# A dynamic-time-warp stage: distances by ScalarE's root and its remainder, rows moved by halves, and the next norm's statistics moved into it

## The reference

```python
def _pairwise_euclidean(a, b):
    aa = jnp.sum(a * a, axis=-1)[:, None]
    bb = jnp.sum(b * b, axis=-1)[None, :]
    ab = a @ b.T
    return jnp.sqrt(jnp.maximum(aa + bb - 2.0 * ab, 0.0))

# _dtw_cost: row i, column j
r = d_ij + jnp.minimum(jnp.minimum(up, left), diag)

# _align_one
expanded = jnp.zeros((T_large, d), dtype=small.dtype).at[j_idx].add(contrib)
```

## Time and profile before

| | |
|---|---|
| median of 3 runs | 1110.68 us (1107.84 to 1112.83) |
| the profiled execution's own time | 1109.92 us |
| its span | 1108.1 us |
| TensorE busy | 863.0 us, 78% |
| VectorE busy | 799.6 us, 72% |
| ScalarE busy | 571.4 us, 52% |
| GpSimd busy | 453.3 us, 41% |
| mean granted TensorE clock | 0.905 |

### The profile page before, as it was taken

One profiled execution on the slowest core, in us unless ns is written; L12 is line 12 of the kernel. 1 busy time (PEld: TensorE's weight loads), 2 busy tenths in 40 slices (PEclk: granted clock), 3 DMA queues, 4 the chain that ended last, 5 costly groups with the idle time before them and its releaser, 6 DMA issues. The chain is left out here.

```text
span 1108.1 us, 25980 instructions
## 1 busy us (share of the span) xinstructions
PE 863.0 (78%) x10175; PEld 617.1 (56%) x10175; DVE 799.6 (72%) x1846; ACT 571.4 (52%) x1299; POOL 453.3 (41%) x288
## 2 busy tenths in 40 slices
PE   4174399689648787179877989898898989868888
PEld 3052254678526566125555767676676767644457
DVE  4889786778764333868879678586958777788964
ACT  3062154467524333456766574647465574346774
POOL 4001130487326665558503363433335262608710
PEclk9687699899759999589989999899999999998989
DMA  5321000400241111200010000000000000000001
GB/s 150 98 62 77 0 1 1 158 2 2 68 161 44 43 44 42 73 1 1 2 49 1 26 2 25 2 25 3 25 4 25 15 13 3 3 1 2 1 2 38
DMA packets 27125, 35.92 MB, mean 32 GB/s; under 512 B 7835, under 2 KB 20444, under 8 KB 26238
## 3 DMA queue, kind: packets, MB, share of 16 engines
q1 hardware_dynamic: 21310, 27.84, 7.9%
q0 software_dynamic: 2496, 5.12, 1.7%
q10 hardware_dynamic: 3200, 1.31, 0.5%
HBM read 26.98 MB, written 7.27 MB: 31 GB/s over the span
## 5 line engine op out<-in xcount | busy, mean ns | idle before, releaser
L1787 PE MATMUL soft_expert_ps<-soft_W,soft_slots 128*32 128x128 f32 x4096 | 139.1, 279 | 14.8 <-issue 8.6
L2058 DVE TENSOR_TENSOR soft_outs<-soft_expert_ps,soft_bias 128x512 f32<-128x512 f32 x128 | 87.2, 687 | 77.2 <-PE soft_expert_ps L1787 77.1
L1787 PEld LDWEIGHTS soft_expert_ps<-soft_W,soft_slots 128*32 128x32 f32 x4096 | 107.2, 111 | 47.2 <-issue 43.3
L925 POOL TENSOR_TENSOR l_prob<-l_prob,l_inv 128x1024 f32<-128x1024 f32 x48 | 91.3, 1901 | 53.4 <-DVE l_inv L1069 53.0
L1879 ACT ACTIVATE soft_slots<-soft_slot_ps 128x512 f32<-128x512 f32 x128 | 69.3, 593 | 81.6 <-PE soft_slot_ps L1773 79.8
L1960 POOL TENSOR_TENSOR l_ring<-l_ring,soft_inv 128x1024 f32<-128x1024 f32 x15 | 39.0, 2629 | 109.4 <-DVE soft_inv L2051 57.7
L1054 DVE TENSOR_REDUCE l_under<-l_score 128x16 f32<-128x1024 f32 x48 | 58.4, 1217 | 32.3 <-PE l_score L1132 14.4
L952 PE MATMUL l_turned<-ident,l_prob 128*128 128x128 f32 x384 | 56.4, 293 | 20.7 <-POOL l_prob L925 20.6
L1736 PE MATMUL soft_slot_ps<-phi,xnT 128*128 128x256 f32 x256 | 66.0, 415 | 7.5 <-ACT soft_spread L1867 5.6
L1960 POOL TENSOR_TENSOR soft_spread<-soft_spread,soft_inv 128x1024 f32<-128x1024 f32 x16 | 41.3, 2610 | 74.0 <-DVE soft_inv L2051 74.0
L1801 PE MATMUL soft_mix_ps<-soft_outs,soft_combT 128*64 128x128 f32 x1024 | 70.0, 279 | 1.5 <-DVE soft_acc L2074 1.5
(11 more groups left out here) (429 smaller groups left out, 2198.2 us busy)
## 6 DMA issues: line engine op xcount, KB each, us to landing
moe_w<-in_moe_W SPq DMA_DIRECT2D x2, 2048.0 KB, 10.0
soft_W<-in_soft_W SPq DMA_DIRECT2D x16, 256.0 KB, 2.7
kept<-early SPq DMA_DIRECT2D x1, 2048.0 KB, 6.3
l_keys<-in_moe_b SPq DMA_DIRECT2D x1, 2048.0 KB, 8.5
l_asked<-kept SPq DMA_DIRECT2D x1, 2048.0 KB, 13.2
ctxT<-in_ctxT SPq DMA_DIRECT2D x1, 1024.0 KB, 5.3
moe_rows<-xn_tok SPq DMA_DIRECT2D x4, 256.0 KB, 3.7
expert_rings<-moe_back SPq DMA_DIRECT2D x4, 256.0 KB, 5.4
```

The source lines that it names most:

```text
L925: nc.gpsimd.tensor_tensor(prob[t % 4][:], prob[t % 4][:], inv[t % 2][:].unsqueeze(2).broadcast_to(S16), ALU.mult).then_inc(share_done, 1)
L1787: last = nc.tensor.matmul(expert_ps[c][32 * j:32 * j + 32, h, tt, :], slots[u % 3][:, h, tt, 128 * c + 32 * j:128 * c + 32 * j + 32], W[i ...
L2058: nc.vector.tensor_tensor(outs[u % 3][:, c].rearrange("p h t d -> p (h t) d"), expert_ps[c][:].rearrange("p h t d -> p (h t) d"), bias[i % ...
```

## The change

- The matmuls that open the banks take bf16 operands.
- ScalarE clamps the distances (relu with scale -2), takes the root and squares the root. VectorE no longer clamps or floors, and has no reciprocal: it gets the inverse of the root from its bits by an integer multiply-add and a refining step, and corrects the root by what its square leaves of the distance, all half by half.
- The minimum for the scan's reset is made ahead of the rows, into a tile of its own. The stop mask is written to `leave`.
- The path's mask is made in two halves of eight tiles, and TensorE waits for the half it needs. A group of four tiles is moved into one whole bank, with four banks for four groups, and added in one operation over 128 partitions.
- The statistics of the next norm are taken behind each group's addition, in `warp`. `bit_ffn` takes one root, one reciprocal and one shift for all 16 tiles.
- For the first four tiles of `bit_ffn`, VectorE instead of GpSimd takes the lift off.

```diff
+INVERSE = float(0x7EF311C3)
...
             for k in range(2):
+                own = slice(8 * k, 8 * k + 8)
+                act.wait_ge(dist_done, k + 1)
+                nc.scalar.activation(dist2[:, own, :], dist_ps[k][:], ACT.Relu, scale=-2.0).then_inc(dist2_done, 1)
                 act.wait_ge(dist2_done, k + 1)
-                nc.scalar.activation(root[:, 8 * k:8 * k + 8, :], dist2[:, 8 * k:8 * k + 8, :], ACT.Sqrt).then_inc(root_done, 1)
+                nc.scalar.activation(root[:, own, :], dist2[:, own, :], ACT.Sqrt).then_inc(root_done, 1)
+                act.wait_ge(root_done, k + 1)
+                nc.scalar.activation(square[:, own, :], root[:, own, :], ACT.Square).then_inc(square_done, 1)
...
-                    nc.tensor.matmul(dist_ps[k][S * h:S * h + S], core.zero[:].broadcast_to([128, S]), ctxT[:, 0:512],
-                                     start=True, stop=False)
+                    nc.tensor.matmul(dist_ps[k][S * h:S * h + S], core.zero[:].bitcast(BF16)[:, 0:1].broadcast_to([128, S]),
+                                     core.ident16[:].unsqueeze(1).broadcast_to([128, 4, 128]), start=True, stop=False)
...
-            pe.wait_ge(path_done, 1)
             for g in range(G):
+                pe.wait_ge(path_done, g // 2 + 1)
                 for k in range(4):
                     t = 4 * g + k
-                    if k == 0 and g >= 2:
-                        pe.wait_ge(added, 2 * g - 2)
                     for h in range(2):
                         half = slice(S * h, S * h + S)
-                        last = nc.tensor.matmul(moved[2 * (g % 2) + h][half, k, :], path[half, t, :], core.ctx_tok[half, t, :],
+                        last = nc.tensor.matmul(moved[g][half, k, :], path[half, t, :], core.ctx_tok[half, t, :],
                                                 start=True, stop=True)
...
+                s, a, q, r, c = (tile[:, own, :] for tile in (root, dist2, square, inv, cost))
                 dve.wait_ge(root_done, k + 1)
-                nc.vector.tensor_scalar_max(inv[:, half, :], root[:, half, :], 1e-30).then_inc(floor_done, 1)
-                dve.wait_ge(floor_done, k + 1)
-                nc.vector.reciprocal(cost[:, half, :], inv[:, half, :]).then_inc(inv_done, 1)
-                dve.wait_ge(inv_done, k + 1)
-                nc.vector.tensor_tensor(inv[:, half, :], dist2[:, half, :], cost[:, half, :], ALU.mult).then_inc(ratio_done, 1)
-                dve.wait_ge(ratio_done, k + 1)
-                nc.vector.tensor_tensor(cost[:, half, :], inv[:, half, :], root[:, half, :], ALU.add).then_inc(cost_done, 1)
+                nc.vector.tensor_scalar(bits(r), bits(s), -1.0, INVERSE, ALU.mult, ALU.add).then_inc(cost_step, 1)
+                dve.wait_ge(cost_step, n + 1)
+                nc.vector.tensor_tensor(c, s, r, ALU.mult).then_inc(cost_step, 1)
+                dve.wait_ge(square_done, k + 1)
+                nc.vector.tensor_tensor(q, q, a, ALU.subtract).then_inc(cost_step, 1)
+                dve.wait_ge(cost_step, n + 2)
+                nc.vector.scalar_tensor_tensor(r, c, 2.0, r, ALU.subtract, ALU.mult).then_inc(cost_step, 1)
+                dve.wait_ge(cost_step, n + 4)
+                nc.vector.tensor_tensor(c, q, r, ALU.mult).then_inc(cost_step, 1)
+                n += 5
+                dve.wait_ge(cost_step, n)
+                nc.vector.scalar_tensor_tensor(c, s, 2.0, c, ALU.mult, ALU.add).then_inc(cost_done, 1)
...
+            dve.wait_ge(dist_done, 2)
+            columns = core.columns[:].unsqueeze(1).broadcast_to([128, R, S])
+            nc.vector.tensor_scalar_min(cut, columns, 1.0).then_inc(first_cut, 1)
...
-            nc.vector.tensor_scalar_min(stops[:], columns, 1.0).then_inc(first_cut, 1)
...
+            for k in range(2):
+                own = slice(8 * k, 8 * k + 8)
+                columns = core.columns[:].unsqueeze(1).broadcast_to([128, 8, S])
+                nc.vector.tensor_tensor(within[:, own, :], columns, exits_ps[:, 1, own].unsqueeze(2).broadcast_to([128, 8, S]),
+                                        ALU.is_le).then_inc(within_done, 1)
+                nc.vector.tensor_tensor(path[:, own, :], columns, exits_ps[:, 0, own].unsqueeze(2).broadcast_to([128, 8, S]),
+                                        ALU.is_ge).then_inc(within_done, 1)
+                dve.wait_ge(within_done, 2 * k + 2)
+                nc.vector.tensor_tensor(path[:, own, :], path[:, own, :], within[:, own, :], ALU.mult).then_inc(path_done, 1)
             for g in range(G):
                 dve.wait_ge(moved_done, g + 1)
-                for h in range(2):
-                    half = slice(S * h, S * h + S)
-                    xs = core.x[half, 4 * g:4 * g + 4, :]
-                    nc.vector.tensor_tensor(xs, moved[2 * (g % 2) + h][half], xs, ALU.add).then_inc(added, 1)
+                xs = core.x[:, 4 * g:4 * g + 4, :]
+                nc.vector.tensor_tensor(xs, moved[g][:], xs, ALU.add).then_inc(added, 1)
+                dve.wait_ge(added, g + 1)
+                for t in range(4 * g, 4 * g + 4):
+                    last = nc.vector.bn_stats(stats[:, t, :], core.x[:, t, :])
+                last.then_inc(measured, 1)
+                dve.wait_ge(measured, g + 1)
+                for t in range(4 * g, 4 * g + 4):
+                    nc.vector.bn_aggr(core.bit_meanvar[:, t, :], stats[:, t, :])
...
-            for t in range(T):
+            for t in range(4, T):
                 pool.wait_ge(in_lifted, 5 * (t // 4) + t % 4 + 2)
...
-            deviate(0)
-            deviate(1)
+            nc.scalar.activation(std[:], meanvar[:, :, 1], ACT.Sqrt, bias=core.eps[:, 0:1]).then_inc(std_done, 1)
             normalise(0)
-            deviate(2)
-            deviate(3)
...
+            def settle(t):
+                dve.wait_ge(in_lifted, t + 2)
+                nc.vector.tensor_scalar(xs[:, t, :], lifted[:, t, :], ROUND, in_scale[:, t:t + 1], ALU.subtract, ALU.mult).then_inc(xs_done, 1)
...
-            statistics(0)
-            statistics(1)
+            dve.wait_ge(std_done, 1)
+            nc.vector.reciprocal(rstd[:], std[:]).then_inc(rstd_done, 1)
+            dve.wait_ge(rstd_done, 1)
+            nc.vector.scalar_tensor_tensor(shift[:], meanvar[:, :, 0], -1.0, rstd[:], ALU.mult, ALU.mult).then_inc(shift_done, 1)
             normalise(0)
             quantise(0)
-            statistics(2)
-            statistics(3)
+            for t in range(4):
+                settle(t)
             normalise(1)
             quantise(1)
```

54 lines of the change are left out of this document (15 added, 39 removed).

## The result

The changed kernel takes 1101.92 us (median of five runs, 1100.16 to 1104.62), beside 1110.2 us (1107.84 to 1112.83) for the kernel before: a ratio of 0.9927, 95% interval 0.9907 to 0.9947. The forecast was 1102.8 us. The profiled execution took 1100.28 us with a span of 1098.5 us, 9.6 us less than before; TensorE's mean granted clock was 0.913 beside 0.905.

A forecast was written before the change was run, and what follows sets the result against it. VectorE's chain was taken to bound most of 19 to 142 us, TensorE the `bit_ffn` loop after. Costs 4.05 + cut 0.7 − tail 0.2 + head 3.4 = 7.95 us off 1109.92; as a median 1102.8 us, range 1098.0 to 1107.0.

The forecast's parts named there:

- The bound: From 19 to 142 us one engine at a time, mostly VectorE, carries the chain; its shift carries to the end.
- Zeroing: Opening matmuls in bf16: half the passes go, worth 0.4 us before the first half of distances, 0.4 before the second.
- Relu, root, square: Distances on ScalarE: each operation takes 0.60 us, and the first root is there at 26.2 us.
- that rival: At the Relu: table loads of 1.28 us, two per half; gain 2.8, time 1104.0; chance 0.13 with fully serial collision.
- The costs: VectorE's cost stage: 3.75 us per half, ending at 35.85 with the collision; worth 4.05 us.
- The collision: VectorE's cost operations meet GpSimd's bias splits from 26.2 us on; 2.1 us lost.
- The rival without a collision: Cost stage: VectorE gets in first and GpSimd waits; 2.1 us more gain, 1100.7 us; chance 0.17.
- The bounds: Cost stage: the meeting with GpSimd loses between 0 and 2.8 us (all serial).
- The cut: The scan's minimum goes from behind the rows to under the wait for `mine` ahead of them; gain 0.7 us.
- The tail: From E, the interval masks' start, to the last aggregation: four groups end at E + 11.9; costs 0.2 us.
- The head: Start of `bit_ffn`: TensorE begins 4.8 us after the start instead of 8.2; gain 3.4 us.
- the third rival: Start of `bit_ffn`: TensorE's low clock gives back 1.7 to 3.4 us of the head; 1104.5 to 1106.2; chance 0.15.

The follow-up runs named there:

- e7_delay: Changed kernel with two more idle VectorE reciprocals (3.35 us each) ahead of the last cost operation; 1091.82 us, ratio 0.9968.
- e6_again: Repeat: changed kernel with GpSimd's memset behind its bias splits and statistics of groups 2 and 3 in `bit_ffn`; 1095.94 us, ratio 0.9867.
- e2_no_collision: Changed kernel with GpSimd's big memset moved behind its bias splits; 1099.69 us, ratio 0.9917.
- e3_stats_back: Changed kernel with all statistics of the next norm back in `bit_ffn`, in groups of four; 1102.55 us, ratio 0.9933.
- e4_split_statistics: Changed kernel with only groups 0 and 1 measured in `warp`, groups 2 and 3 in `bit_ffn`; 1099.37 us, ratio 0.9894.

## Why the prediction was right, point by point

- *The bound.* VectorE's chain to E and the head behind it set the time, and the shift passes on: e7_delay showed it with 6.5 us for 6.39. The loop of `bit_ffn` ran at its clock of 1.00 and passed the shift on.
- *Zeroing.* Expected 0.4 ahead of the first half and 0.4 more before the second. The second is 0.64; the first is 0.49 in one pair of executions, within a spread of 2.5 us, so it isn't shown. That most of it would be eaten by the collision wasn't in the sum. The first Relu at 24.93 (24.8) fits, by some luck: the same code started it between 22.14 and 25.95.
- *Relu, root, square.* 0.60, 0.63 and 0.63, first root at 26.19 (26.2). No table load, so that rival is dead. The Trainium skill (ScalarE: Activation LUTs, Table sets) has relu in every set, and this trace agrees for the set that was loaded: no load stands between Relu, root and square.
- *The costs.* A half is 3.73 us from its start to the next one's where nothing collides (3.75; e6_again), the integer form is the fast one (0.42), and the second bank isn't waited for. The collision is 1.95 to 2.05 us (2.1), by e2_no_collision and e6_again. The end came at 35.80 (35.85); gain 4.10 for 4.05. The rival without a collision is refuted by the rows; its price, 2.1, was right.
- *Which end of the bounds.* The row of the walk back, 0.67 lost of 0.91, was a good price list: 2.03 us summed over the excess of the four stretched operations of the first half (0.39, 0.84, 0.40, 0.40). The bounds held for a start at 26.2 only: in e3_stats_back, which starts at 23.43, more of GpSimd's work lies ahead, and the two halves take 10.72 us, 3.2 over the undisturbed 7.53.
- *The cut.* −0.72 from the costs' end to E (0.7), but only 0.53 of it lies between the first row and E, where the minimum stood; 0.19 is a shorter way from the costs' end to the first row, 4.99 us where other executions have 4.87 to 5.32. Over all kernels with the cut, the first row to E is 0.53 to 0.80 us shorter than before. The minimum now lies at 39.89 under a wait for `mine` of which 0.22 us is left.
- *The tail.* Masks at E + 2.01 (2.05), first addition at E + 4.17 (4.1), 1.90 per group (1.93), end at E + 11.86 (11.9).
- *The head.* Transposes 4.66 us behind the block's first instruction (4.8). Told from VectorE's first instruction, as the signs had it, it is 4.32; the 4.8 had counted ScalarE's root in. Tail and head together gave 3.41 (3.2).
- *Given back.* That is the term that the sum left out and the third rival had, at 1.7 to 3.4 us: TensorE begins earlier but at the lower level, and the first `bit_up` takes 5.05 us instead of 4.05. The rise didn't stay at its absolute time, as that rival had it, but came 6.2 us earlier. What was given back is 1.0 in this pair, and by the spread of the last column of the table it could have been 0 to 1. The sum also left out the 0.72 us that the early shift gains inside the loop. The two nearly cancel: 8.23 at the transposes, less 1.00, plus 0.72, is the 7.95 that leaves the loop. That this equals the sum of 7.95 to the hundredth is luck.
- *One sentence was wrong.* "What VectorE's statistics of tiles 8 to 15 took there was hidden under a wait for ScalarE" saw only VectorE. In ScalarE's queue their roots stood ahead of the copy of the transposed tile, and e3_stats_back showed 1.36 us for it once the transposes come early. And the 1.93 us per group in the tail were booked as the price of something needed at once, while only half of it was: e4_split_statistics got 2.7 us of it back. That "their removal gives nothing more" was wrong as well: the 0.72 us in the loop come with it.
- *The time.* Profile against profile the gain is 9.6 us, median against median 8.3, and the sum was 7.95. The stretch up to the end of the loop explains 7.95. Behind it the two profiles are between 4.4 us (at 451 us of before) and 9.6 us (from 549 us on, to the end) apart, and they change in stages that the change doesn't touch. So what is beyond the sum there isn't explained, and is within the spread of single executions. The forecast of 1102.8 against 1101.92 is closer than such executions repeat (1100.16 to 1104.62), so the last microsecond of the agreement is luck.

## What to carry to other kernels

Before an engine is given a chain of short two-operand operations in place of one long one, look at what GpSimd does in the same microseconds: the time of the meeting is to be added operation by operation. Here, moving a memset on GpSimd gave back the 2 us that the new arithmetic had lost to it. Work that is taken forward should be taken forward only as far as its first reader needs it, here two groups of four, and the queue of every engine that takes part is to be read, not the moved engine's alone. Where an edit is worth 1 to 3 us in 1100, compare marks in the trace relative to a mark that both kernels share, since the times of whole executions can't tell it.

## What the runs showed of the hardware that wasn't expected

- A GpSimd copy on a single partition (1x512, 0.60 us alone) holds up VectorE's operations on 128 partitions by 0.34 to 0.40 us, and is itself stretched to 0.95 us. A VectorE reciprocal of 3.35 us isn't held up at all.
- VectorE's multiply-add on int32 (128x512) takes 0.42 us, as long as the fp32 one.
- The pace of the distances' TensorE stretch changes between executions of the same code: its first cost operation starts between 23.43 and 27.25 us. The profile grants 1.00 in windows from 16 to 28 us, though the same 128x64 matmul takes 0.48 us at 21 us and 0.34 at 25 in one of them; here the granted clock doesn't tell the pace, and why is open. The end of the costs varies less, 34.15 to 36.69, since an early start meets more of GpSimd's work.
- E to the first transposes repeats to 0.02 us over seven kernels, while whole executions of one kernel differ by 2 to 9 us.
